# Moving the second Gram product, the weight loads, the token sums and one small op in an attention and feed-forward kernel

## The reference

```
x = layernorm(x)                              # x: 16 x 2048 x 1024
mu, var = mean(x), var(x);  h = (x-mu)/sqrt(var+eps) * norm_w + norm_b
q, k, v = split(h @ qkv_w.T + qkv_b)          # one head
w = softmax(q^T k * scale, over k)            # 1024 x 1024: over channels
a = (w applied to v) @ proj_w.T + proj_b + x
x1 = x_in + a
out = x1 + ffn(layernorm(x1))                 # 1024 -> 4096 -> 1024,
```

## Time and profile before

| | us |
|---|---|
| median of 3 runs | 1492.59 (1492.22 to 1492.6) |
| profiled execution | 1493.21 |
| its span, core 0 (slowest; the others from 1483.7) | 1491.6 |

### The profile page before, as it was taken

How to read it: one execution, slowest core, us unless ns; L and a number is a source line. 1 busy time by engine, 2 the same in 40 slices (tenths; PEclk the granted TensorE clock), 3 DMA queues, 4 the chain that set the end, 5 groups by cost and what they waited for, 6 DMA issues and landing times.

```text
span 1491.6 us, 22343 instructions; the slowest of 8 cores (1483.7 to 1491.6 us)
## 1 busy us (share of the span) xinstructions
PE 1348.3 (90%) x6232; PEld 603.7 (40%) x6232; DVE 1114.7 (75%) x1696; ACT 806.0 (54%) x1294; POOL 604.8 (41%) x411
## 2 busy tenths in 40 slices
PE   4697979888999767789999999999999999999998
PEld 2342435433344322234444444444444444444443
DVE  7525871592423779989889888888888888888884
ACT  3512450452223455676676666676766766666660
POOL 3533252351346437743443433433443443443340
PEclk9998998999999999999999999999999999999999
DMA  7997461479997765212003004003003003002002
GB/s 241 282 250 216 150 205 41 143 259 226 266 267 259 252 232 195 60 24 70 30 15 99 29 15 100 29 15 99 29 15 100 30 15 99 30 15 71 29 15 92
DMA packets 124542, 171.96 MB, mean 115 GB/s; under 512 B 74620, under 2 KB 74620, under 8 KB 124420
## 3 DMA queue, kind: packets, MB, share of 16 engines
q1 hardware_dynamic: 124420, 170.52, 38.6%
HBM read 103.38 MB, written 50.33 MB: 103 GB/s over the span
## 4 chain that ended last, share of the span: by engine, by line
PE 48%; DVE 20%; issue 16%; DMA 8%; ACT 4%; SPq 3%; DVEq 1%; POOL 1%; ACTq 0%; POOLq 0%
PE pf L611 15%; PE pf L639 9%; PE pf L624 8%; DVE gb L911 6%; DVE rbits L903 4%; DMA x1scr<-xo 4%; PE pf L423 3%; PE pf L451 3%; DVE rbits L914 3%; PE pf L366 2%; DVE ub L928 2%; SPq L221 2%; DVE bn L686 2%; PE pf L395 2%; PE pf L502 2%
## 5 line engine op out<-in xcount | busy, mean ns | idle before, releaser
L1183 POOL TENSOR_TENSOR gb<-gb,ga 128x512 f32<-128x512 f32 x256 | 362.6, 1416 | 525.3 <-ACT gb L1132 525.3
L624 PE MATMUL pf<-w,yt 128*128 128x512 bf16 x1024 | 258.2, 380 | 50.7 <-ACT yt L1120 33.5
L914 DVE SCALAR_TENSOR_TENSOR rbits<-ga,gb 128x512 int32<-128x512 f32 x256 | 268.3, 1048 | 27.5 <-DVE gb L911 0.9
L1120 ACT ACTIVATE yt<-rbits 128x512 bf16<-128x512 int32 x256 | 160.8, 628 | 208.9 <-DVE rbits L914 208.9
L639 PE MATMUL pf<-w,yt 128*128 128x512 bf16 x1024 | 252.7, 381 | 0.0
L611 PE MATMUL pf<-z2cmA,w 128*128 128x512 bf16 x1024 | 242.3, 380 | 1.5 <-ACT kb L1112 1.5
L611 PE MATMUL pf<-z2cmB,w 128*128 128x512 bf16 x1024 | 241.9, 379 | 0.0
L1112 ACT ACTIVATE kb<-pf,b1x 128x512 int32<-128x512 f32 x256 | 173.5, 678 | 94.8 <-PE pf L611 93.6
L911 DVE SCALAR_TENSOR_TENSOR gb<-rbits,gb 128x512 f32<-128x512 int32 x256 | 196.1, 766 | 3.3 <-POOL gb L1183 3.3
L903 DVE TENSOR_SCALAR rbits<-kb 128x512 int32<-128x512 int32 x256 | 150.5, 588 | 48.8 <-ACT kb L1112 47.9
L1132 ACT ACTIVATE gb<-kb,c 128x512 f32<-128x512 int32 x256 | 181.0, 707 | 0.0
(11 more groups left out here) (91 smaller groups left out, 1156.1 us busy)
## 6 DMA issues: line engine op xcount, KB each, us to landing
ring<-xs SPq DMA_DIRECT2D x64, 512.0 KB, 5.0
ring<-w_h SPq DMA_DIRECT2D x64, 512.0 KB, 8.2
x1scr<-xo SPq DMA_DIRECT2D x32, 512.0 KB, 5.5
xh<-x1scr SPq DMA_DIRECT2D x64, 256.0 KB, 3.3
ys<-xh SPq DMA_DIRECT2D x64, 256.0 KB, 2.4
zscr<-Z SPq DMA_DIRECT2D x32, 256.0 KB, 2.8
z2scr<-z2b SPq DMA_DIRECT2D x32, 256.0 KB, 2.7
ring<-wq_h SPq DMA_DIRECT2D x8, 512.0 KB, 9.4
```

The lines of the kernel that those rows point to most:

```text
L624: mm = t.matmul(bank(tt), y_tile(c, ft, tt), w2[:, ft, 0:512], start=(ft == 0), stop=(ft == 31))
L914: v.scalar_tensor_tensor(out=rbits[n % 4][:], in0=ga[n % 2][:], scalar=256.0, in1=gb[n % 2][:], op0=ALU.mult, op1=ALU.add).then_inc(S["v_h ...
L1120: a.activation(out=yt[:, r, q, :, :] if c % 2 == 0 else yt[:, r, :, q, :], in_=rbits[e % 4][:].rearrange("p (a b) -> p a b", a=4), func=AF ...
L1183: g_.tensor_tensor(out=gb[n % 2][:], in0=gb[n % 2][:], in1=ga[n % 2][:], op=ALU.subtract).then_inc(S["g_d"], 1)
```

## The change

- **Loads ahead of stores.** SyncE issues every x load of sequence 0, four wq tiles among them, then the other wq and all wk tiles, before the first store of z. A function `wait_slot` finds the wait that a ring position needs. ScalarE casts four wq tiles between normalised tiles; wk is cast on ScalarE, two tiles behind each of its T1 evictions 8, 10, 12 and 14, no longer on GpSimd. The rest of the load order (six p tiles, `load_zt`, two p tiles, wv) stays.
- **Token sums later.** `accumulate(0)` starts after tile 16. `col_sums(1)` comes after two groups of the second Gram product.
- **Second Gram product** in nine portions: two ahead of output tile 0, one ahead of each of the tiles 1, 2, 3, 4, 6, 7 and 8 of output stage 0, in the banks `LO`, with their evictions on VectorE ahead of the same tile's `x1_tile`. Its transposes and mirrors move from the tiles 1 and 3 to 10 and 12.
- **T1 of sequence 1** is evicted in rising order of d, each pair of tiles waiting only for the store of the `xo` buffer that it overwrites, and not for all four.
- **`nms2` on GpSimd.** In iteration m GpSimd adds the row of tile m+2 and then makes `nms2` of tile m-1 (`g_nms2`).
- A `Sqrt` of one column at the start of ScalarE's program.

```diff
+G_BANK = [[0, 1, 2, 3, 7, 6, 0, 5, 4], [2, 3, 1, 2, 3, 0, 1, 2, 3]]
+G_SLOTS = [[0], [1, 2], [3, 4], [5, 6], [7], [8], [9], [10], [11]]
+OUT0_SLOTS = {0: [0, 1], 1: [2], 2: [3], 3: [4], 4: [5], 6: [6], 7: [7], 8: [8]}
...
+def x_pos(t):
+    return t if t < 8 else t + (t - 6) // 2
+
+
+def q_pos(j):
+    return 8 + 3 * j if j < 4 else 16 + j
+
+
+X_AT = {x_pos(t): t for t in range(16)}
+Q_AT = {q_pos(j): j for j in range(8)}
...
+            def wait_slot(u):
+                p = u - 6
+                if p in X_AT:
+                    s.wait_ge(S["a_z"], X_AT[p] + 1)
+                elif p in Q_AT:
+                    s.wait_ge(S["a_wq"], Q_AT[p] + 1)
+                elif p < U_P:
+                    s.wait_ge(S["a_wk"], p - U_WK + 1)
...
             def load(u, src):
+                if u >= 6:
+                    wait_slot(u)
...
             for t in range(6):
-                load(U_X0 + t, x_tile(t))
+                load(x_pos(t), x_tile(t))
             for dst, src in ((ident[:], ident_h), (cols[:], cols_h), (c2[:], c2_h)):
                 s.dma_start(out=dst, in_=src).then_inc(S["d_const"], 16)
+            for t in range(6, 16):
+                load(x_pos(t), x_tile(t))
+                if t in (7, 9, 11, 13):
+                    load(q_pos((t - 7) // 2), wq_h[(t - 7) // 2])
+                if t == 10:
+                    s.dma_start(out=nwb[:], in_=nwb_h).then_inc(S["d_nwb"], 16)
+            for j in range(4, 8):
+                load(q_pos(j), wq_h[j])
+            for j in range(8):
+                load(U_WK + j, wk_h[j])
+            s.dma_start(out=bq2[:], in_=bq2_h).then_inc(S["d_rows"], 16)
+            s.dma_start(out=bk2[:], in_=bk2_h).then_inc(S["d_rows"], 16)
             for t in range(16):
                 s.wait_ge(S["a_z"], t + 1)
                 store_z(t)
...
             s.dma_start(out=nbb[:], in_=nbb_h).then_inc(S["d_nbb"], 16)
             s.dma_start(out=rbb[:], in_=pbb_h).then_inc(S["d_pb"], 16)
+            for j in range(6):
+                load(U_P + j, p_h[j])
             s.wait_ge(S["d_zst"], 256)
             load_zt(0)
+            for j in range(6, 8):
+                load(U_P + j, p_h[j])
             for j in range(8):
+                load(U_WV + j, wv_h[j])
+            for t in range(6):
+                load(U_X1 + t, x_tile(16 + t))
...
-            wait_n_slot(0, 10)
-            col_sums(1, 2)
-
-
-            for idx in range(12):
-                if idx in (0, 1, 3, 5, 7, 8, 9):
-                    wait_n_slot(0, [11, 12, 0, 13, 0, 14, 0, 15, 16, 17][idx])
-                elif idx == 10:
+
+
+            def gram_slot(k):
+                if k < 3:
+                    wait_n_slot(0, [10, 11, 17][k])
+                elif k == 5:
                     t.wait_ge(S["v_sc"], 2)
-                elif idx == 11:
-                    t.wait_ge(S["v_g"], 13)
-                for c in range(16):
-                    t.wait_ge(S["a_z"], 16 + c + 1)
-                    mm = g_mm(1, idx, c, start=(c == 0), stop=(c == 15))
-                mm.then_inc(S["pe_g"], 1)
-
-            wait_n_all(0)
+                else:
+                    t.wait_ge(S["v_g"], 12 + {3: 1, 4: 3, 6: 5, 7: 7, 8: 8}[k])
+                for idx in G_SLOTS[k]:
+                    for c in range(16):
+                        if k == 0:
+                            t.wait_ge(S["a_z"], 16 + c + 1)
+                        mm = g_mm(1, idx, c, start=(c == 0), stop=(c == 15))
+                    mm.then_inc(S["pe_g"], 1)
+
             for m in range(16):
-                if m in (0, 1):
-                    t.wait_ge(S["v_g"], 12 + [5, 8][m])
+                for k in OUT0_SLOTS.get(m, []):
+                    gram_slot(k)
+                if m == 0:
+                    wait_n_slot(0, 16)
+                    col_sums(1, 0)
+                    wait_n_all(0)
                 out_tile(0, m)
-                if m == 1:
+                if m == 10:
                     t.wait_ge(S["v_g"], 24)
                     for j in (7, 6, 5, 4):
                         transposes(1, j)
-                if m == 3:
+                if m == 12:
                     t.wait_ge(S["a_tr"], 7 + 4)
                     for j in (3, 2, 1):
                         transposes(1, j)
...
             def x1_scale(g):
                 v.wait_ge(S["a_sd2"], g + 1)
                 v.reciprocal(out=sr2[:, g:g + 1], in_=sd2[:, g:g + 1]).then_inc(S["v_sr2"], 1)
-                v.wait_ge(S["v_sr2"], g + 1)
-                v.scalar_tensor_tensor(out=nms2[:, g:g + 1], in0=mv2[:, g, 0:1], scalar=-1.0, in1=sr2[:, g:g + 1],
-                                       op0=ALU.mult, op1=ALU.mult).then_inc(S["v_nms2"], 1)
...
             def out_stage(b):
                 for m in range(16):
+                    if b == 0:
+                        for k in OUT0_SLOTS.get(m, []):
+                            gram_evict(1, k)
+                        if m == 0:
+                            columns(1, 0)
                     x1_tile(b, m)
                     if m >= 1:
                         x1_scale(16 * b + m - 1)
...
-                h, d = i // 8, 7 - i % 8
+                h, d = i // 8, 7 - i % 8 if b == 0 else i % 8
+                if b == 1 and h == 0:
+                    v.wait_ge(d_x1st[d // 2], 64)
+                    v.wait_ge(S["a_z2"], 12 + d // 2 + 1)
                 v.wait_ge(S["pe_t1"], 16 * b + i + 1)
...
             for i in range(8, 16, 2):
                 t1_evict(0, i)
+                cast(wk[:, i - 8, :], U_WK + i - 8, "a_wk")
+                cast(wk[:, i - 7, :], U_WK + i - 7, "a_wk")
             exponentials(0)
...
         def gpsimd_program(g_):
             def accumulate(b):
-                if b == 1:
+                if b == 0:
+                    g_.wait_ge(S["a_z"], 16)
+                else:
                     g_.wait_ge(S["v_w"], 8)
...
+            def add_row(b, m):
+                g = 16 * b + m
+                g_.wait_ge(S["a_tl"], g + 1)
+                g_.tensor_tensor(out=xo[g % 4][:], in0=xo[g % 4][:], in1=rbb[:], op=ALU.add).then_inc(S["g_rb"], 1)
+
+            def out_stage(b):
                 g_.wait_ge(S["v_rb"], 2 * (b + 1))
+                add_row(b, 0)
+                add_row(b, 1)
+                for m in range(17):
+                    if m + 2 < 16:
+                        add_row(b, m + 2)
+                    if m >= 1:
+                        g = 16 * b + m - 1
+                        g_.wait_ge(S["v_sr2"], g + 1)
+                        g_.tensor_scalar(out=nms2[:, g:g + 1], in0=mv2[:, g, 0:1], scalar1=sr2[:, g:g + 1],
+                                         scalar2=-1.0, op0=ALU.mult, op1=ALU.mult).then_inc(S["g_nms2"], 1)
```

More of the change, by code:

```diff
@@ L177, in build_program @@
         ones = small("ones", [128, 1])
+        warm = small("warm", [128, 1])
         pf = E(nc.psum_tensor("pf", [128, 4096], F32))
@@ L294, in out_stores @@
                     s.dma_start(out=z2scr[128 * g:128 * (g + 1), :], in_=z2b[g % 2][:]).then_inc(d_z2st[g % 2], 16)
[L295 to L299, removed]
+            out_stores(0)
+            for k in range(6):
+                load(U_W1 + k, w1_h[k])
             s.wait_ge(S["pe_out"], 16)
@@ L307, in sync_program @@
             load_zt(1)
-            for k in range(26):
-                s.wait_ge(S["g_w1"], k + 1)
-                load(U_W1 + k + 6, w1_h[k + 6])
+            for k in range(6, 32):
+                load(U_W1 + k, w1_h[k])
             s.wait_ge(S["pe_s"], 16)
@@ L874, in vector_program @@
             finish_stats(31)
-            columns(1, 2)
-            gram_evict(1)
             residual_scales(1)
             out_stage(0)
-            for i in range(4):
-                v.wait_ge(d_x1st[i], 64)
-            v.wait_ge(S["a_z2"], 16)
             for i in range(1, 16, 2):
@@ L952, in scalar_program @@
             a.wait_ge(S["v_set"], 1)
+            a.activation(out=warm[:], in_=ceps[:], func=AF.Sqrt)
             def std(g):
@@ L1051, in out_stage @@
                 for m in range(17):
+                    if b == 0 and m == 11:
+                        for j in (7, 6, 5, 4):
+                            mirror(1, j)
+                    if b == 0 and m == 13:
+                        for j in (3, 2, 1):
+                            mirror(1, j)
                     if m + 2 < 16:
@@ L1057, in out_stage, with cast @@
                         normalise2(b, 16 * b + m - 1)
-                    if b == 0 and m == 2:
-                        for j in (7, 6, 5, 4):
-                            mirror(1, j)
-                    if b == 0 and m == 4:
-                        for j in (3, 2, 1):
-                            mirror(1, j)
+            def cast(dst, u, sem):
+                landed(a, u)
+                a.activation(out=dst, in_=ring[u % 6][:], func=AF.Copy, scale=1.0).then_inc(S[sem], 1)
             for g in range(17):
@@ L1068, in scalar_program @@
                 if g >= 1:
```

(12 more changed lines are left out.)

127 lines of the change are left out of this document (48 added, 79 removed).

## The result

The changed kernel took 1510.82 us (median of 4 executions, 1510.01 to 1514.12) against 1492.59: ratio 1.0127 [1.0109 to 1.0144], 18 us slower. The forecast was 1494, the range ended at 1506.

What follows compares the result with a forecast made beforehand. Before 550 us it took holes in TensorE's work as the bound: normalisation, queued loads before the scores, token sums, output-stage store chains. Terms 11 - 19 + 9 = +1 on 1493.2 us gave 1494, range 1483 to 1506.

Steps and rivals of the forecast that it cites:

- Part 1: Loads ahead of stores, sums later: first `wv` product and scores of sequence 0 come later, +11 us, bounds +5 to +15.
- Rival D: SyncE's queue does not bite: first `wv` lands as before, term 1 at 0 or below; 1483 us, chance 0.11.
- the price of the late token sums: Additions end at 81 us, where sums are wanted after T1 tile 11: no cost, 30 us of cover if late.
- Part 2: Second Gram product between output tiles of stage 0: T1 of sequence 1 resumes sooner, -19 us, bounds -28 and -15.
- the cover that was named: Output stage 0: residual tiles and additions run ahead during Gram; tiles 10 to 15 partly live on that, 31 us taken.
- Part 3: `nms2` on GpSimd behind the addition: output stage 1's loop turns get longer, +9 us, bounds +1 to +14.
- 4 x 1.6 + 3: Output stage 1: four turns between fourth and twelfth store, 1.6 us longer each, first turns losing some 3 us; +9.
- Rival C: Handover of `nms2` costs in full, landing 6.3 or more, `nms2` 0.6, stage 0 loses 3 us; 1502 us, chance 0.27.
- Rival B: VectorE's held time was part of the output loop; its relief pays back the handover, term 3 0 to +1; 1486, chance 0.17.

Runs made afterwards that it cites:

- stores_first: The changed kernel with SyncE issuing the 16 stores of z ahead of the wk loads; 1490.3 to 1496.9 us, ratio 0.9987 to the kernel before.
- after: The whole change against the kernel before, on the chip of the result; 1510.82 us, ratio 1.0127.
- after_again: The unaltered changed kernel run again on chip C, beside the kernel before; 1502.11 us, ratio 1.0052.
- gram_alone: The kernel before with only the second Gram product between output tiles and T1 evictions in rising order; 1463.2 to 1464.2 us, ratio 0.9802.
- nms_back: The changed kernel with `nms2` made on VectorE again, GpSimd left with its additions; 1478.79 us, ratio 0.9890 to the kernel before.
- nms_first: The changed kernel with GpSimd making `nms2` of m-1 ahead of the addition of m+2; 1474.22 us, ratio 0.9867 to the kernel before.
- after_third: The unaltered changed kernel run a third time, on chip D, against the kernel before; 1500.01 us, ratio 1.0041.
- zt_late: The changed kernel with sequence 0's transposing loads behind all `wv` loads; 1474.8 to 1478.7 us, 1489.8 to 1490.9 with a low-clock pair; ratio 0.9927 to before.
- front_alone: The kernel before with only the new load/store order, wk casts on ScalarE, late token sums and early `Sqrt`; 1506.65 to 1527.36 us, ratio 1.0149.
- fill: The changed kernel plus 130 useless matmuls in TensorE's stop before the scores; 1505.44, 1502.19 and 1501.35 us, ratio 1.0062 to the kernel before.

## Why the prediction was wrong

**Part 1.** The numbers came close, but not by the path that I gave. Last tile 46.9 (forecast 49), first T1 eviction 56.86 (59.5), hole 60 to 77 (the same), transposes 94.31 (93 to 95), first product 135.23 on core 0 (138). Core 0 gained on its forecast, the mean of the cores didn't: +13 to +14.5 against +11, inside +5 to +15. Rival D had no part in it. The step that failed is the price of the late token sums, "nothing, and 30 us of cover if they are late". The additions end at 81.05, as forecast, but TensorE had been idle for them for 4.25 us, and it works in order: T1 tiles 12 to 15 come behind the column sums, the last four casts of wk behind those tiles, and the fifth and sixth p tile behind the casts. With the stores as they are, SyncE stands for this on core 0 only from 91.06 to 92.94, so there it costs some 2 us, an estimate; with the stores out of the way (`stores_first`) it alone holds the transposing loads to 96 us. That they came when the sum of the stores said they would is luck in part: two paths end at about the same time. Of the 13.3 us by which the first product of `after` is late in the mean, 9.0 are the later issue of the transposing loads and 4.6 their longer hold on the queue, which the prediction had as unchanged. No run has the late sums alone, so how the 9.0 divides stays open. The cure was one line away, since the wait is for `wv` and the transposes could stand behind it.

**Part 2.** The term was -19 with output stage 0's handover of `nms2` in it. Measured up to the last T1 matmul, `after_again`: 221.2 - 244.3 = -23.1, inside -28 to -15. Without the handover it is -28.5 (`gram_alone`), and in the company of the Gram product the handover costs 5.8 (`nms_back`) instead of the 10.1 it costs alone: the cover that was named is there, for about half.

**Part 3.** This term of the sum is mis-sized: +9 forecast, bounds +1 to +14, measured +14.3 up to the last `z2b` (190.4 - 176.1), just outside. The order of waits was right: `z2b` 4.1 us behind its residual, turn 11.8 with a landing of 5.5, measured 11.9 with 5.4. What failed is the count, "4 x 1.6 + 3". The starts of the residual tiles of output stage 1, means over the cores, show it:

| residual tiles | before | after_again | forecast |
|---|---|---|---|
| 0 to 3 | 9.3 | 9.3 | +3 |
| 3 to 13, five turns | 50.8 | 60.6 | four turns of +1.6 |
| 13 to 15 | 6.9 | 11.0 | +0 |
| 15 to the last `z2b` | 9.8 | 10.0 | +0 |

There are five turns, not four, each 2.0 us longer, and the first turns lose nothing. The last pair of tiles loses 4.1 us, for which I had no term. In the chain above it waits for no store (523.44 to 534), and I let it be as fast as before. But the handover closes a loop of its own, residual, addition, `nms2`, `z2b`, next residual, on two in-order engines: 5.47 us for each tile, and 2 x 5.47 is the 11.0. Once that loop runs, no residual tile can come faster. Adding the pieces of the earlier trace rows once around (1.24 + 2.35 + 0.3 for the op + 1.22 = 5.1) would have shown it, since the tiles had come at 67.2 / 15 = 4.5 us on average before. `nms2` itself was 0.27 us, the 0.3 taken. Rival C's 1502 had nearly the right time, but by a landing of 6.3 that did not come. Rival B's relief of VectorE is real and small: `nms_first` against `nms_back`, 5.3 us over both stages (on two chips), and only once the addition no longer stands ahead of `nms2`.

**Sum.** The forecast of +1 us was 11 - 19 + 9. In the columns of the table `after_again` has 14.5 - 23.1 + 14.3 + 0.7 = +6.4, and `after_third` 5.8; the slowest core, by the medians, 8 and 6. Without a low pair the kernel is at 1500 to 1502, inside 1483 to 1506 and on the side of "slower".

**The clock.** The rest, 9 to 11 us on the slowest core, had no term in the sum, and without it the time is inside the range, as chips C and D show. The trace of before shows no core at 0.81, and nothing in it would have given a price. The Trainium skill (TensorE: Matmul & The Clock Gate, section Seeing it yourself, on the peak-current limiter) names such a clock, 13/16 of the full one, once three cores of a die run dense matmuls, and says that it takes the whole die. The 0.81 agrees. That a single pair takes it differs: from 160 to 200 us cores 4 and 5 had 0.81 while the die's other two had 1.00, and the measurement decides.

## What to carry to other kernels

When a small op moves to an engine that works in order, add up the loop it closes, engine by engine and once around, and not only the wait that it puts into the old loop; then put it ahead of the large op, not behind it (23 to 28 us here, with it ahead or back on VectorE). When loads and transposing loads share a queue, issue first what the next product needs (24 us here, 18 to 22 once `nms2` is mended). When sums move to a later place, ask what stands behind their consumer on its in-order engine, and which queue waits for that. And with eight cores, look at the granted clock of every core before a difference of 1% is put down to the code: the same kernel was 1.3% slower on one chip and 0.4 to 0.5% on two others.

## What was not expected of the hardware

Two neighbouring cores can fall to a granted clock of 0.81 for 80 to 130 us, while the other two of their die have 1.00 (cores 4 and 5 against 6 and 7 of `after`, 160 to 200 us). It came at changing places, on the chip of the result and on chip A, and not on B, C or D; with it the slowest core took 14 to 20 us more in `zt_late` and `front_alone`. Eight transposing loads of one and the same size kept SyncE's queue for 25.7 us in `stores_first` and 32.6 us in `after`; why, no run shows. 130 matmuls added in TensorE's stop cost nothing measurable (`fill` 1494.8 against 1494.1 of `after_again` in the mean span). A dependent 128x1 op on GpSimd took 0.27 us, hardly more than the 0.16 us on an undisturbed VectorE.
